# The first two pairs of a Strassen-Winograd kernel on one core: transfers in order of use, sums and riding columns on VectorE, an order of its own for pair 1, J7 waiting for T4 by halves

## The reference

```python
x = x + einsum('bct,bcd->bdt', x, cond_w[cond_idx])          # 128 x 128 per sequence
H = einsum('btd,od->bto', x, W)                              # W is 1024 x 1024
xa = einsum('btd,brd->btr', x, A[adapter]);  delta = einsum('btr,bor->bto', xa, Bm[adapter])
x = x + H + delta * scalings[adapter]
```

## Time and profile before

| | |
|---|---|
| median of 3 runs | 792.66 us (792.52 to 794.56) |
| profiled execution, its own time | 792.67 us |
| its span | 790.9 us |
| mean granted TensorE clock | 0.999 |
| TensorE busy (matmul) | 775.4 us, 98% |
| VectorE, ScalarE, GpSimd busy | 525.9, 384.2, 142.7 us |

### The profile page before, as it was taken

The page is one execution under the profiler, slowest core; times in us unless marked ns, Lnnn a source line. Parts: engine busy times, 40 slices in busy tenths (PEclk is TensorE's granted clock), DMA queues, the critical chain, the costliest instruction groups (busy, mean ns, idle before and its releaser), DMA issues.

```text
span 790.9 us, 16285 instructions
## 1 busy us (share of the span) xinstructions
PE 775.4 (98%) x5219; PEld 720.5 (91%) x5219; DVE 525.9 (66%) x923; ACT 384.2 (49%) x722; POOL 142.7 (18%) x304
## 2 busy tenths in 40 slices
PE   5989999999999999999999999999999999999998
PEld 5879999999999999999999999999999999999996
DVE  6896677666776666766666776666766667666664
ACT  6464454454454544454544444444544444545443
POOL 3831221201212102121011212012121021211000
PEclk9999999999999999999999999999999999999999
DMA  8343234332234332343322333322343323333202
GB/s 288 112 152 100 90 127 142 128 118 77 101 134 139 106 124 69 119 139 133 112 103 86 123 139 133 113 81 101 130 139 111 130 66 110 139 136 109 80 35 106
DMA packets 45623, 92.55 MB, mean 117 GB/s; under 512 B 7588, under 2 KB 24228, under 8 KB 45604
## 3 DMA queue, kind: packets, MB, share of 16 engines
q1 hardware_dynamic: 45314, 92.04, 33.8%
q10 hardware_dynamic: 290, 0.27, 0.2%
HBM read 58.72 MB, written 33.55 MB: 117 GB/s over the span
## 4 chain that ended last, share of the span: by engine, by line
PE 95%; DVE 3%; DMA 1%; ACT 0%; issue 0%; POOL 0%; SPq 0%; POOLq 0%
PE beta L935 34%; PE delta L951 22%; PE beta L948 11%; PE alpha L935 11%; PE o_ps L987 4%; PE o_ps L988 4%; PE o_ps L986 4%; PE delta L963 2%; PE alpha L966 1%; PE beta L1084 1%; PE beta L966 1%; PE alpha L1084 1%; PE delta L1094 1%; DMA w_raw<-wB 1%; DVE wr_lo L844 1%; PE o_ps L1094 0%
## 5 line engine op out<-in xcount | busy, mean ns | idle before, releaser
L407 POOL TENSOR_TENSOR wr_lo<-a_ride,wr_hi 128x192 fp32r<-128x192 f32 x31 | 19.1, 616 | 562.1 <-ACT wr_hi L492 562.1
L935 PE MATMUL beta<-wr_hi,s_hi 128*128 128x256 f32 x496 | 101.4, 286 | 1.3 <-ACT v_sb L523 0.7
L935 PE MATMUL beta<-wr_hi,s_lo 128*128 128x256 f32 x496 | 101.1, 285 | 0.0
L935 PE MATMUL beta<-wr_lo,s_hi 128*128 128x256 f32 x496 | 101.0, 285 | 0.0
L951 PE MATMUL delta<-wn_hi,s_hi 128*128 128x512 f32 x248 | 99.1, 400 | 0.0
L951 PE MATMUL delta<-wn_hi,s_lo 128*128 128x512 f32 x248 | 97.3, 393 | 0.0
L951 PE MATMUL delta<-wn_lo,s_hi 128*128 128x512 f32 x248 | 96.9, 391 | 0.0
L821 DVE COPY o_sb<-o_ps 128x512 f32<-128x512 f32 x60 | 41.3, 688 | 76.6 <-PE o_ps L988 76.6
L935 PEld LDWEIGHTS beta<-wr_hi,s_hi 128*128 128x128 f32 x496 | 79.8, 189 | 4.2 <-ACT v_sb L523 0.9
L935 PEld LDWEIGHTS beta<-wr_lo,s_hi 128*128 128x128 f32 x496 | 77.9, 188 | 0.0
L935 PEld LDWEIGHTS beta<-wr_hi,s_lo 128*128 128x128 f32 x496 | 77.6, 188 | 0.0
(11 more groups left out here) (235 smaller groups left out, 1903.6 us busy)
## 6 DMA issues: line engine op xcount, KB each, us to landing
out<-o_sb SPq DMA_DIRECT2D x60, 512.0 KB, 2.8
x_even<-xT SPq DMA_DIRECT2D x32, 512.0 KB, 4.1
x_odd<-xT SPq DMA_DIRECT2D x30, 512.0 KB, 4.1
b_raw<-lora_b SPq DMA_DIRECT2D x192, 64.0 KB, 2.1
a_now<-lora_a SPq DMA_DIRECT2D x64, 64.0 KB, 2.4
c_raw<-cond_w SPq DMA_DIRECT2D x64, 64.0 KB, 1.8
w_raw<-wB SPq DMA_DIRECT2D x4, 512.0 KB, 6.8
w_raw<-wB SPq DMA_DIRECT2D x4, 256.0 KB, 4.9
```

Of the source, the lines that this page charges most:

```text
L407: nc.gpsimd.tensor_tensor(ride_of(wr_lo, J1, J2), a_ride[:, :, 0:3, :], ride_of(wr_hi, J1, J2), ALU.subtract).then_inc(ride_ready, 1)
L935: last = nc.tensor.matmul(bank[:, h, 0:hi - lo], left[:, chunk + k, :], right[:, k, lo:hi], start=opens and k == 0 and left is left_hi and ...
```

## The change

It touches only the opening, that is pairs 0 and 1. `step` for all later pairs issues what it issued before.

- **Transfers.** SyncE loads in the order of use: the first half of x of sequence 0 in one piece, B11 in three pieces (chunk 0, chunk 1, chunks 2 and 3), then x of sequence 1 and the scalings, both of which ScalarE's queue had issued.
- **TensorE** does all of sequence 0 with the left half of B11 first, then sequence 1. The last condition product of pair 0 (`times_c` to `o_ps[1]`) moves from behind J2 of pair 1 to behind its J4. J7 waits for T4 by halves.
- **VectorE** takes over what GpSimd did with the identities, with A's scaling and with T3. T2 is summed earlier, T3 later.
- **GpSimd** only picks the scalings, until pair 2.
- **Pair 1 has orders of its own** (`first_step`) on ScalarE and VectorE.

```diff
-            load_first_x(0, 0, 2, 0)
-            load_b11(0)
-            load_b11(1)
-            load_first_x(0, 2, 2, 1)
-            load_b11(2)
+            load_first_x(0, 0, 0)
+            for n, k in enumerate((slice(0, 1), slice(1, 2), slice(2, 4))):
+                sp.dma_start(w_a[:, k, :], wB[B11, :, k, :]).then_inc(w_landed[B11][n], 16)
+            load_first_x(1, 0, 1)
+            sp.dma_start(s_tab[:, :], scalings.to_broadcast([P, NAD])).then_inc(s_landed, 16)
...
-            load_b11(3)
...
+            load_w(w_c, B12)
...
-            pool.wait_ge(b22_added, 1)
-            pool.wait_ge(w_lo_ready, M12)
-            pool.wait_ge(t1_summed, 2)
-            sum_t3(0)
-            rest_ride(0, 0, 1)
-            for k in range(1, KH):
-                sum_t3(k)
+            pick_scalings(0, 0, 0)
+            pool.wait_ge(a_scaled, 4)
+            pick_scalings(0, 0, 1)
+            pool.wait_ge(a_scaled, 8)
+            pool.wait_ge(ride_ready, 4)
+            step(0, 1)
...
+            def first_step():
...
+                act.wait_ge(j2_done, 1)
+                act.wait_ge(first_stored, 48)
+                nc.scalar.activation(q1_sb[:, :, :], halves(beta), ACT.Copy).then_inc(q1_ready, 1)
+                act.wait_ge(s3_summed, 1)
+                nc.scalar.activation(s3_hi[:, :, :], x_raw[slot][:, 1, 0:KH, :], ACT.Copy).then_inc(s3_hi_ready, 1)
+                for half in range(2):
+                    act.wait_ge(t3_summed, half + 1)
+                    hi_of(wr_hi[:, :, J6 * RS:J6 * RS + H], w_c, half)
+                hi_of_b(i, j)
+                act.wait_ge(j4_done, 1)
+                nc.scalar.activation(as_halves(v_sb[:, :]), halves(beta), ACT.Copy).then_inc(v_ready, 1)
+                evacuate_first(flat(c22_sb[:, :, :]), o_ps[1][:, :], 4)
+                act.wait_ge(s1_summed, 1)
+                nc.scalar.activation(s1_hi[:, :, :], s1_raw[:, :, :], ACT.Copy).then_inc(s1_hi_ready, 1)
+                for half in range(2):
+                    act.wait_ge(t4_summed, half + 1)
+                    hi_of(wn_hi[:, J7, :, :], w_b, half)
+                hi_of_a22(i, j)
+                hi_of_s4(i, j)
+                split_x1(i, j, 1)
+                act.wait_ge(j6_done, 1)
+                act.wait_ge(xa_ready, 2)
+                act.wait_ge(first_stored, 64)
+                nc.scalar.activation(c22_sb[:, :, :], halves(beta), ACT.Copy).then_inc(c22_begun, 1)
+                turned_xa(i, j)
+                ride(i, j, 1)
...
             act.wait_ge(first_product, 7)
             nc.scalar.activation(flat(s2_hi[:, :, :]), delta[:, :], ACT.Copy).then_inc(first_z_hi, 1)
             split_x1(0, 0, 1)
+            hi_of_t2(1)
+            act.wait_ge(first_product, 8)
+            nc.scalar.activation(flat(s1_hi[:, :, :]), o_ps[1][:, :], ACT.Copy).then_inc(first_z_hi, 1)
             evacuate_first(v_sb[:, :], o_ps[0][:, :], 1)
-            act.wait_ge(first_product, 8)
-            nc.scalar.activation(flat(s3_hi[:, :, :]), o_ps[1][:, :], ACT.Copy).then_inc(first_z_hi, 1)
             evacuate_first(flat(c22_sb[:, :, :]), xaT_ps[:, :], 2)
             evacuate_first(flat(q1_sb[:, :, :]), alpha[:, 0, :], 3)
             split_s2(0, 0, 1)
-            act.wait_ge(first_product, 6)
-            for half in range(2):
-                act.wait_ge(t2_summed, half + 1)
-                hi_of(wr_hi[:, :, J4 * RS:J4 * RS + H], w_a, half)
+            first_step()
...
+            def first_step():
+
+                i, j = 0, 1
+                rest_s3(i, j)
+                rest_of(MT3, wr_lo[:, :, J6 * RS:J6 * RS + H], w_c, wr_hi[:, :, J6 * RS:J6 * RS + H])
+                sum_t4(0)
+                rest_s1(i, j)
+                sum_t4(1)
+                first_xa_of(i, j)
+                rest_b(i, j)
+                split_xa_first(i, j)
+                split_xa_second(i, j)
+                rest_a22(i, j)
+                rest_of(MT4, wn_lo[:, J7, :, :], w_b, wn_hi[:, J7, :, :])
+                sum_s4(i, j)
+                rest_s4(i, j)
+                sum_c22(i, j)
+                sum_c11(i, j)
+                rest_x1(i, j, 1)
+                sum_s1(i, j, 1)
+                sum_s3(i, j, 1)
+                sum_s2(i, j, 1)
+                rest_z22(i, j)
+                rest_z11(i, j)
+                add_identity_c(i, j)
+                rest_c(i, j)
+                rest_z21(i, j)
+                rest_s2(i, j, 1)
+
...
+            scale_ride(0, ((3, 0, 0), (4, 1, 0), (0, 0, KH), (1, 1, KH)))
+            rest_of_b11(0, 2, 1, 4)
+            rest_of_b11(2, 2, 1, 5)
+            rest_last_ride(1)
+            beside = slice(J1 * RS + H, J1 * RS + H + 2 * R)
+            dve.wait_ge(ride_hi_ready, 2)
+            nc.vector.tensor_tensor(wr_lo[:, :, beside], a_ride[:, :, 0:2, :].rearrange("p k s r -> p k (s r)"),
+                                    wr_hi[:, :, beside], ALU.subtract).then_inc(ride_ready, 1)
...
+            for half in range(2):
+                add_identity_b22(half)
+            rest_of_first_x(a22_lo[:, :, :], 1, KH, a22_hi[:, :, :], 3)
             rest_of(MT1, wn_lo[:, J3, :, :], w_a, wn_hi[:, J3, :, :])
+            dve.wait_ge(ride_ready, 2)
+            scale_ride(1, ((0, 0, KH), (4, 0, 0), (1, 1, KH), (3, 1, 0)))
+            dve.wait_ge(a_scaled, 8)
+            nc.vector.tensor_tensor(a_ride[:, :, 2, :], a_ride[:, :, 1, :], a_ride[:, :, 3, :], ALU.subtract)\
+                .then_inc(a_summed, 1)
+            add_identity_c(0, 0)
             rest_of(M22, wn_lo[:, J5, :, :], w_d, wn_hi[:, J5, :, :])
+            sum_t2(0)
...
+            rest_b(0, 0)
+            sum_t2(1)
             rest_c(0, 0)
...
+            rest_of(MT2, wr_lo[:, :, J4 * RS:J4 * RS + H], w_a, wr_hi[:, :, J4 * RS:J4 * RS + H])
             dve.wait_ge(x_landed[0], 32)
             sum_s1(0, 0, 1)
             sum_s3(0, 0, 1)
             sum_s2(0, 0, 1)
-            rest_of_first_z(4, flat(s3_lo[:, :, :]), o_ps[1][:, :], flat(s3_hi[:, :, :]))
-            dve.wait_ge(w_lo_ready, MT1)
+            rest_s2(0, 0, 1)
+            part_of_xa(0, 1)
+            dve.wait_ge(t1_summed, 2)
+            dve.wait_ge(b22_added, 2)
             for half in range(2):
-                nc.vector.tensor_tensor(two(w_a, half), two(w_d, half), two(w_a, half), ALU.subtract)\
-                    .then_inc(t2_summed, 1)
-            rest_s2(0, 0, 1)
-            rest_of(MT2, wr_lo[:, :, J4 * RS:J4 * RS + H], w_a, wr_hi[:, :, J4 * RS:J4 * RS + H])
+                nc.vector.tensor_tensor(two(w_c, half), two(w_d, half), two(w_c, half), ALU.subtract)\
+                    .then_inc(t3_summed, 1)
+            rest_of_first_z(4, flat(s1_lo[:, :, :]), o_ps[1][:, :], flat(s1_hi[:, :, :]))
+            first_step()
...
                     riding(beta, x1_hi, x1_lo, 0, J2, 2, True).then_inc(j2_done, 1)
                     if first:
                         pe.wait_ge(first_out, 3)
-                        pe.wait_ge(first_z, 4)
-                        times_c(o_ps[1][:, :], 1, flat(s3_hi[:, :, :]), flat(s3_lo[:, :, :])).then_inc(first_o, 1)
...
                     if first:
                         pe.wait_ge(w_lo_ready, MT2)
                     riding(beta, s2_hi, s2_lo, 0, J4, 1, False).then_inc(j4_done, 1)
+                    if first:
+                        pe.wait_ge(first_z, 4)
+                        times_c(o_ps[1][:, :], 1, flat(s1_hi[:, :, :]), flat(s1_lo[:, :, :])).then_inc(first_o, 1)
...
+                if exists(i, j, -1):
+                    plain(beta, a22_hi, a22_lo, J7, False)
+                else:
+                    plain(beta, a22_hi, a22_lo, J7, False, half_of_t4)
                 lora(beta, g_second, 0).then_inc(beta_done, 1)
+
+            def half_of_t4(k):
+                if k % 2 == 0:
+                    pe.wait_ge(w_lo_ready, MT4 - 1 + k // 2)
...
-            for k in range(2):
-                pe.wait_ge(w_lo_ready, k + 1)
+            for k in range(KH):
+                if k < 3:
+                    pe.wait_ge(w_lo_ready, k + 1)
                 first_left(k, 0, alpha, x1_hi, x1_lo, True, J2)
-            pe.wait_ge(first_x_ready, 3)
-            for k in range(2):
-                first_left(k, 0, beta, s1_hi, s1_lo, True, J2)
-            for k in range(2, KH):
-                pe.wait_ge(w_lo_ready, k + 1)
-                first_left(k, 0, alpha, x1_hi, x1_lo, True, J2)
+            pe.wait_ge(first_x_ready, 2)
+            for k in range(KH):
                 first_left(k, 0, beta, s1_hi, s1_lo, True, J2)
```

432 lines of the change are left out of this document (226 added, 206 removed).

## The result

The changed kernel takes 795.62 us (median of 20 runs, 794.75 to 796.46). The kernel before, timed beside it, takes 794.35 us (20 runs, 792.52 to 795.60). The medians differ by 1.3 us; the ratio worked out over all these runs is 1.0024, with a 95% interval of 1.0017 to 1.0031. So the change makes the kernel slower by 1.3 to 2.5 us. The forecast was 794.8 us, the range 792.4 to 797.0.

What follows compares the result with a forecast made beforehand. TensorE, busy 775.4 of 790.9 us, was taken as the bound, with VectorE setting the pace in pair 1. Pair 2 starting at 66.5 instead of 64.33 adds 2.15 to 792.66: 794.8 us, range 792.4 to 797.0.

Steps and rivals of the forecast that it cites:

- The frame: From pair 2 on TensorE's order is unchanged: time after is time before plus that start's shift, 2.15 us.
- The lead: Opening: TensorE has eighteen matmuls left at 9.5 us instead of 10.53, a lead of 1.0 us (bounds 0 and 1.6).
- VectorE's list: VectorE through pair 1: starts about 13.0 us, x low part 34.75, T3's sums 41.5, S4's sum ends 56.0.
- GpSimd beside VectorE: Pair 1: GpSimd's four scalings slow VectorE's instructions, adding 0.4 us up to the end of S4's sum.
- the full block: GpSimd's four scalings block VectorE for their whole time: S4's sum 3.6 us later, 798.4 us; chance 0.02.
- The wait for `g_second`: Pair 1: TensorE stands still 5.0 us because S4's sum comes last on VectorE; it goes on at 58.45 us.
- From there to pair 2: TensorE goes from 58.45 us to pair 2 at 66.5, including 1.4 us of waiting for Z21's low part.
- The clock: TensorE's matmuls turn slow behind pair 1's long wait: +0.9 to +2.2 us, 795.7 to 797.0 us; chance 0.15.
- The base: Time before taken as 792.66 us, from the profiled execution's 792.67 less 0.01.
- the forecast's bound: Whole kernel: about 0.3% (2.4 us) counts as no change, so slower begins above 795.05 us.
- The other side: Pair 1: the wait for S4 does not bind, three gaps and the opening's gain save 4.1 us: 788.6; chance 0.08.

Runs made afterwards that it cites:

- experiment 3: The changed kernel with 20 extra matmuls of 512 columns on TensorE ahead of its wait for `g_second`, results unread: 795.44 us, ratio to before 1.0021.
- 4: The kernel before with only pair 1's S4 sum moved late on VectorE, directly ahead of S4's low part: 795.73 us, ratio to before 1.0025.
- 5: The kernel before with 44 extra matmuls of 128 columns from the identity's arrival on: 795.14 us, ratio to before 1.0021.
- 6: The changed kernel with 30 extra matmuls of 128 columns from the identity's arrival on: 797.38 us, ratio to before 1.0046.
- experiment 8: The kernel before, unchanged, profiled and timed again: 793.38 us, ratio to before 0.9997.
- experiment 9: The kernel before with 10 extra matmuls of 512 columns ending ahead of the first real one: 793.54 us, ratio to before 0.9997.
- experiment 10: The changed kernel with 7 extra matmuls of 512 columns ahead of its first real one: 795.36 us, ratio to before 1.0018.
- experiment 11: The changed kernel with J7 waiting for both halves of T4's low part at once: 795.42 us, ratio to before 1.0018.
- Experiments 1: The changed kernel with pair 1's S4 sum moved early on VectorE, between S2's sum and S2's low part: 793.36 us, ratio to before 0.9991.
- Version 2: The changed kernel with S4's sum early, Z21's low part ahead of pair 2's sums and its high part ahead of C's: 789.71 us, ratio to before 0.9947.

## Why the prediction was right, point by point

**The frame held.** The time after is the time before plus the shift of pair 2's start: from there to the end it took 726.4 to 726.6 us in the traces of both kernels and of 3 to 6 and 8 to 11.

**The lead.** TensorE ran without a gap from 9.53 us (forecast 9.5), with the eighteen matmuls left. The slow stretch ended at 13.4 us and not at 15.0, so the lead had grown to 1.3 us by the first matmul of pair 0's last two products (28.34 against 29.61). Between there and the adapters' product 0.6 of it was lost, of which 0.18 is a wait for `b_stack`. At J2 it was 0.65 us, not 1.0 (37.69 against 38.34). It changed nothing, as was said.

**VectorE's list.** In the profiled execution it began at 13.99 us, a microsecond later than the 13.0 of the forecast, because ScalarE waited longer for a piece of W; so pair 1's x came at 35.50, T3's sums at 42.19 and S4's sum ended at 56.60. In experiment 11 it began at 13.03, and the same three are 34.74, 41.45 and 56.21, against 34.75, 41.5 and 56.0 forecast. The list was sized rightly. Its start moves by 1.4 us from execution to execution (12.60 in experiment 3), pair 1's x by less (34.88 there).

**GpSimd beside VectorE.** I had added 0.4 us up to S4's sum and gave the full block 2 in 100. In the profile only the low part of B is longer beside GpSimd's four scalings: 0.15 us (1.37 instead of the 1.22 of the earlier trace rows). In experiments 3 and 11 three instructions are: half of T4's sum (1.35 and 1.32 instead of 1.22), the low part of B (1.37) and a small xa instruction (0.34 instead of 0.18). That is 0.4 us, the term as it was forecast. The Trainium skill (SBUF — State Buffer, "SBUF: two separate sides") has whichever engine is later wait for the other's instruction; no row of pair 1 shows VectorE held for a whole scaling (0.75 us in the profile, where the four took 3.00). The 0.78 in place of 0.69 appears behind this stretch, at three instructions ahead of Z21.

**The wait for `g_second`.** Forecast: 5.0 us, ending at 58.45. Measured: 4.86 ending at 59.09 in the profile, 4.84 ending at 58.72 in experiment 11. Experiments 1 and 4 show the cause from both sides: without S4's sum in that place the wait goes, and with nothing but it the kernel before becomes as slow as the changed one, in its trace half of it by the clock that falls behind the longer wait.

**From there to pair 2,** the term that was too small. I had 8.05 us from `g_second` to pair 2, 1.4 of it waiting for Z21. Experiment 3, where the clock stays up, has 8.63 (67.41 - 58.78), 1.78 of it waiting; experiment 11 has 8.84. VectorE's part from C22's sum to the end of Z21's low part was 7.45 in the forecast and is 7.87 in experiment 3 (59.39 to 67.26): three rows of 0.78 beside GpSimd add 0.3, the identity at 0.51 another 0.1. C22's sum starts 0.61 us behind the adapters' product there, and 0.87 in experiment 11, where that product is slow; the forecast had 0.47. With `g_second` 0.3 us late as well, pair 2 begins at about 67.5, not 66.5. With the earlier trace rows and 726.5 that is some 794.0 of span and 795.8 us, 0.2 above the measured median. The late `g_second` and this term together are the 0.8 us by which the forecast was short.

**The clock.** The rival had 0.15, and its mechanism is what happens: in every trace of the changed kernel with that wait left idle (the profile, 6, 10 and 11) matmuls behind it are slow for 3 to 6 us. The Trainium skill (TensorE: Matmul & The Clock Gate, Part 1) says that an idle array goes back to half rate, and after 4.9 us these traces agree. TensorE's own work from `g_second` to pair 2 is 6.85 us in experiment 3 (8.63 less the wait of 1.78). It is 8.4, 9.1 and 9.4 in experiment 11, the profile and experiment 10, so the slow stretch takes 1.5 to 2.5 us of TensorE. But pair 2 moves only from 8.63 to 8.84, 9.10 and 9.37 us, by 0.2 to 0.7; the rest hides behind Z21, and the medians of the changed kernel and of experiment 3 differ by 0.2. The rival's price at pair 2, 0.9 to 2.2 us, was too high. So forecast and rival were no alternatives. Both held at once, and one hid the other.

**The base.** The forecast took 792.66 us as the time before. On that base its shift was too small: 2.15 us forecast, 3.2 and 3.9 in the starts of pair 2 (experiment 11 and the profile against 64.33), 3.0 in the median after. The ratio over all runs gives 1.9 us (0.0024 of 794.35), close to 2.15, but that is luck: more runs put the median before at 794.35, and the higher base offsets the term that was too small. The line between "same" and "slower" moves with the base too: 795.62 lies above the forecast's bound of 795.05 and below 0.3% over 794.35. Of the 20 runs of before nine lie at 792.9 in the mean and eleven at 794.8; from the one the difference is 2.7 us, from the other 0.8.

What makes the second value is open. Beside the experiments and in experiment 8 the kernel before ran 96 times. None of the 38 executions with a mean granted clock of 0.999 or 1.000 took over 793.9 us, and all 40 over 794 had 0.998 or less, but so had 18 below 794. So a fallen clock goes with the upper group and is not enough for it. The fall behind xa's wait of 1.8 to 1.9 us is a candidate: experiment 9 shows it, both traces of before and 5 do not. Yet the execution in which it was seen is not one of the longer ones of its own kernel, and no execution of before above 794 us has a trace. The opening can differ as well: two traces of before are 0.7 us apart at J2 of pair 1 (38.34 and 39.02). That the changed kernel has one group only would fit the candidate, since its wait is so long that the clock falls each time; this is not shown.

**The other side.** "The wait for S4 does not bind" would have given 788.6. Version 2, in which it doesn't and Z21 doesn't either, has 789.7.
